# Packing the register tables of a gather ring: TensorE's slots and landed counts in one word of 30 bits, SyncE's reuse counts three to a word

## What is computed

```python
def _gnn_layer(x, row, col, W, b, g, beta):
    n = x.shape[0]
    neigh = x[col]
    agg = jax.ops.segment_sum(neigh, row, num_segments=n)
    deg = jax.ops.segment_sum(jnp.ones((row.shape[0],), x.dtype), row, num_segments=n)
    deg = jnp.maximum(deg, 1.0)[:, None]
    h = (x + agg / deg) @ W.T + b
    ...
    return jax.nn.silu(hn)
```

## Time and profile before

| what | value |
|---|---|
| median of 3 runs | 3740.51 us (3739.39 to 3745.12) |
| the profiled execution, its own time | 3739.08 us |
| its span, first to last instruction | 3737.3 us |
| TensorE busy / POOL busy | 2240.2 us (60%) / 1554.4 us (42%) |
| granted TensorE clock, mean over the span | 0.785 |

### The profile page before, as it was taken

One profiled execution on the slowest core, in us unless ns is written; L12 is line 12 of the kernel. 1 busy time (PEld: TensorE's weight loads), 2 busy tenths in 40 slices (PEclk: granted clock), 3 DMA queues, 4 the chain that ended last, 5 costly groups with the idle time before them and its releaser, 6 DMA issues.

```text
span 3737.3 us, 36443 instructions
## 1 busy us (share of the span) xinstructions
PE 2240.2 (60%) x9253; PEld 1681.5 (45%) x9253; DVE 1446.4 (39%) x3178; ACT 1600.0 (43%) x3874; POOL 1554.4 (42%) x1637
## 2 busy tenths in 40 slices
PE   0711456656656665568255666575666577079988
PEld 0411234445444454455144445454544465047766
DVE  8577512323333332215413323232333224866611
ACT  6000144445545454554344555454555453423333
POOL 0000166656666656630356656666666620400000
PEclk9955577878777877789577877787777788589979
DMA  4100133333333333321323323333332323200011
GB/s 155 57 0 0 30 89 93 94 90 97 90 92 93 97 87 90 88 64 58 118 85 92 94 88 99 93 92 90 92 94 85 90 72 135 95 26 0 0 82 55
DMA packets 100949, 293.32 MB, mean 78 GB/s; under 512 B 28161, under 2 KB 42319, under 8 KB 94538
## 3 DMA queue, kind: packets, MB, share of 16 engines
q0 software_dynamic: 75264, 205.62, 19.1%
q1 hardware_dynamic: 12524, 73.00, 5.2%
q10 hardware_dynamic: 13000, 12.80, 1.2%
HBM read 259.31 MB, written 32.00 MB: 78 GB/s over the span
## 4 chain that ended last, share of the span: by engine, by line
PE 35%; another core or an unknown queue 23%; DVE 22%; issue 9%; SPq 2%; DVEq 2%; DMA 2%; ACT 2%; POOL 0%; ACTq 0%; PEldq 0%; POOLq 0%
PE ps L929 17%; PE ps L1071 3%; DVE big L1463 3%; PE ps L1053 3%; DVE arena_a L1175 2%; PE ps L1140 2%; DVE arena_a L1176 2%; DVE nodes L1517 2%; PE ps L946 2%; PE ps L1013 1%; DVE big L1567 1%; PE ps L827 1%; DMA nodes<-x_rows 1%; ACT arena_b L592 1%
## 5 line engine op out<-in xcount | busy, mean ns | idle before, releaser
L495 POOL DMA_INDIRECT big<-table,arena_a x1568 | 1508.4, 962 | 1421.7 <-issue 447.0
L929 PE MATMUL ps<-big 128*125 x3968 | 1136.0, 448 | 920.3 <-DVE big L1463 778.6
L929 PEld LDWEIGHTS ps<-big 128*125 128x125 f32 x3968 | 876.7, 226 | 1153.5 <-issue 985.0
L1463 DVE TENSOR_TENSOR big<-ps,big 125x257 f32 x496 | 211.3, 426 | 1732.2 <-remote 976.8
L592 ACT ACTIVATE arena_b<-iota_row,arena_a 128x125 f32<-128x125 f32 x1984 | 601.4, 386 | 37.7 <-ACT nodes L633 14.0
L594 ACT ACTIVATE big<-arena_b,ones 128x1000 f32<-128x1000 f32 x248 | 280.2, 1130 | 22.6 <-remote 11.4
L622 ACT ACTIVATE nodes<-ps 128x750 f32<-128x750 f32 x50 | 39.9, 797 | 330.6 <-remote 328.6
L1517 DVE RECIPROCAL nodes<-nodes 125x512 f32<-125x512 f32 x50 | 167.7, 3353 | 1.7
L649 ACT ACTIVATE nodes<-ps 125x768 f32<-125x768 f32 x50 | 40.3, 806 | 289.8 <-remote 258.8
L946 PE MATMUL ps<-arena_b,nodes 128*125 128x384 f32 x400 | 159.4, 522 | 0.0
L615 ACT ACTIVATE nodes<-nodes 125x512 f32<-125x512 f32 x50 | 31.6, 631 | 260.3 <-issue 166.7
(11 more groups left out here) (362 smaller groups left out, 3018.4 us busy)
## 6 DMA issues: line engine op xcount, KB each, us to landing
big<-table,arena_a POOLq DMA_INDIRECT x1568
nodes<-in_x_dram SPq DMA_DIRECT2D x10, 1250.0 KB
table<-nodes SPq DMA_DIRECT2D x10, 1250.0 KB
nodes<-table SPq DMA_DIRECT2D x10, 1250.0 KB
nodes<-table ACTq DMA_DIRECT2D x50, 125.0 KB
mix_rows<-nodes ACTq DMA_DIRECT2D x50, 125.0 KB
big<-mix_rows SPq DMA_DIRECT2D x5, 1250.0 KB
x_rows<-nodes SPq DMA_DIRECT2D x5, 1250.0 KB
```

Of the source, the lines that this page charges most:

```text
L495: pool.indirect_dma_start(gat[:, GRP * slot + k, 0:D], None, table[l], bass.IndirectOffsetOnAxis(ap=s_dst[:, n:n + 1], axis=0)).then_inc(s ...
L929: mm = pe.matmul(ps[0:PT, 4 + q % 2, 0:257], onehot[:, ROUND * (r % 2) + QS * k + n, :], gat[:, bass.ds(slots[QS * k + n], 1), :].squeeze( ...
L1463: dve.tensor_tensor(at, ps[0:PT, 4 + q % 2, 0:257].unsqueeze(1), at, ALU.add).then_inc(s("agg_added"), 1)
```

## The change

Per quad there is now one word of 30 bits: four ring places of five bits, and above them the landed count of ten. `need_row` and `free_row` hold one layer's numbers; the other layer's share is added to the register. TensorE loads 16 such words at once, at the start of every fourth round, and takes each place out with a shift and a mask. SyncE's table has three counts of eight bits to a word, and 16 words (48 groups) to a load. The order of the engines' work stays as it was.

```diff
@@ -192,10 +192,12 @@
         s_row, o = carve(arena_a, o, [NSL])
         assert o <= 2 * NCK * P - NQ // PACK
         slot_row, o = carve(arena_a, 2 * NCK * P, [NSL], I32, 1)
-        need_row, o = carve(arena_a, o, [2, NQ], I32, 1)
+        quad_row, o = carve(arena_a, o, [NQ], I32, 1)
+        need_row, o = carve(arena_a, o, [NQ], I32, 1)
         tile_row, o = carve(arena_a, o, [NQ], F32, 1)
         pack_row, _ = carve(arena_a, 2 * NCK * P - NQ // PACK, [NQ // PACK], I32, 1)
-        free_row, o = carve(arena_a, o, [2, NGRP], I32, 1)
+        free_row, o = carve(arena_a, o, [NGRP], F32, 1)
+        free_words, o = carve(arena_a, o, [(NGRP - 2) // 3], I32, 1)
         assert o <= 4750 - 5 * (NT + 1)
         away, _ = carve(arena_b, 0, [GRP, PT])
 
@@ -402,13 +404,15 @@
             for l in range(2):
 
                 tell_landed(l, 0)
-                for first in range(0, NGRP - RG, 16):
-                    _, quads_before = nc.values_load_multi_w_load_instructions(
-                        free_row[0:1, l, first:first + 16], [mybir.EngineType.SP], min_val=1, max_val=2 * NQ,
-                        skip_runtime_bounds_check_because="a sum of clamped counts, held to one or more by a maximum before it is stored")
-                    for grp in range(first, min(first + 16, NGRP - RG)):
+                for first in range(0, NGRP - RG, 48):
+                    _, words = nc.values_load_multi_w_load_instructions(
+                        free_words[0:1, first // 3:first // 3 + 16], [mybir.EngineType.SP], min_val=1, max_val=(1 << 24) - 1,
+                        skip_runtime_bounds_check_because="three sums of clamped counts of eight bits, each held to one or more by a maximum")
+                    for grp in range(first, min(first + 48, NGRP - RG)):
                         tell_landed(l, grp + 1)
-                        sp.wait_ge(s("agg_made"), quads_before[grp - first])
+                        k = (grp - first) % 3
+                        quads_before = (words[(grp - first) // 3] >> (8 * k)) & 255
+                        sp.wait_ge(s("agg_made"), (quads_before + NQ * l).with_bounds(min_val=1, max_val=2 * NQ))
                         sp.sem_inc(s("slots_free"), 1)
                 for grp in range(NGRP - RG + 1, NGRP):
                     tell_landed(l, grp)
@@ -910,24 +914,28 @@
             for l in range(2):
                 pe.wait_ge(s("agg_added_credit"), l + 1)
 
-                def products(r, l=l):
-                    _, slots = nc.values_load_multi_w_load_instructions(
-                        slot_row[0:1, r * ROUND:(r + 1) * ROUND], [mybir.EngineType.PE], min_val=0, max_val=RG * GRP - 1,
-                        skip_runtime_bounds_check_because="five bits of a number")
-                    _, needs = nc.values_load_multi_w_load_instructions(
-                        need_row[0:1, l, r * (ROUND // QS):(r + 1) * (ROUND // QS)], [mybir.EngineType.PE], min_val=1, max_val=2 * NGA,
-                        skip_runtime_bounds_check_because="a chunk's number plus one, held to the tile's last by a minimum")
+                quad_words = []
+
+                def products(r, l=l, quad_words=quad_words):
+                    first = r * (ROUND // QS)
+                    if first % 16 == 0:
+                        _, loaded = nc.values_load_multi_w_load_instructions(
+                            quad_row[0:1, first:min(first + 16, NQ)], [mybir.EngineType.PE], min_val=1 << 20, max_val=(1 << 30) - 1,
+                            skip_runtime_bounds_check_because="four slots of five bits, and above them a chunk's number plus one, of ten")
+                        quad_words[:] = loaded
                     for k in range(ROUND // QS):
+                        word = quad_words[(first + k) % 16]
+                        slot = lambda n: ((word >> (5 * n)) & (RG * GRP - 1)).with_bounds(min_val=0, max_val=RG * GRP - 1)
                         q = r * (ROUND // QS) + k + NQ * l
                         if k * QS % GRP == 0:
                             pe.wait_ge(s("onehot_ready"), 2 * r + k * QS // GRP + 1 + NSG * l)
-                        pe.wait_ge(s("landed"), needs[k])
+                        pe.wait_ge(s("landed"), ((word >> 20) + NGA * l).with_bounds(min_val=1, max_val=2 * NGA))
                         if q >= 2:
 
                             pe.wait_ge(s("agg_added"), q - 1)
                         for n in range(QS):
                             mm = pe.matmul(ps[0:PT, 4 + q % 2, 0:257], onehot[:, ROUND * (r % 2) + QS * k + n, :],
-                                           gat[:, bass.ds(slots[QS * k + n], 1), :].squeeze(), start=(n == 0), stop=(n == QS - 1))
+                                           gat[:, bass.ds(slot(n), 1), :].squeeze(), start=(n == 0), stop=(n == QS - 1))
                         mm.then_inc(s("agg_made"), 1)
 
                 def mix_slot(i, l=l):
@@ -1420,12 +1428,21 @@
                                               op0=ALU.mult, op1=ALU.add))
             do.mark(dve.tensor_scalar(slot_row, chunk_row, -1.0, None, ALU.add))
             last_of_quad = chunk_row.rearrange("p (q c) -> p q c", c=QS)[:, :, QS - 1]
-            for l in range(2):
-                do.mark(dve.tensor_scalar(need_row[:, l, :], last_of_quad, float(NGA * l), None, ALU.add))
-                do.mark(dve.tensor_scalar(free_row[:, l, :], ps[0:1, 3, 3 * P:3 * P + NGRP], 1.0, float(NQ * l), ALU.max, ALU.add))
+            do.mark(dve.tensor_copy(need_row, last_of_quad))
+            do.mark(dve.tensor_scalar(free_row, ps[0:1, 3, 3 * P:3 * P + NGRP], 1.0, None, ALU.max))
             do.wait()
-            link(dve.tensor_scalar(slot_row, slot_row, RG * GRP - 1, None, ALU.bitwise_and))
-            link(dve.tensor_copy(pack_row, in_word(tile_row, 0)))
+            do.mark(dve.tensor_scalar(slot_row, slot_row, RG * GRP - 1, None, ALU.bitwise_and))
+            do.mark(dve.tensor_scalar(need_row, need_row, 20, None, ALU.logical_shift_left))
+            do.mark(dve.tensor_copy(pack_row, in_word(tile_row, 0)))
+            in_free = lambda k: free_row[:, 0:NGRP - 2].rearrange("p (w c) -> p w c", c=3)[:, :, k]
+            do.mark(dve.scalar_tensor_tensor(out=in_free(1), in0=in_free(2), scalar=256.0, in1=in_free(1), op0=ALU.mult, op1=ALU.add))
+            do.wait()
+            in_quad = lambda n: slot_row.rearrange("p (q c) -> p q c", c=QS)[:, :, n]
+            do.mark(dve.scalar_tensor_tensor(out=free_words, in0=in_free(1), scalar=256.0, in1=in_free(0), op0=ALU.mult, op1=ALU.add))
+            for n in (2, 1, 0):
+
+                link(dve.scalar_tensor_tensor(out=in_quad(n), in0=in_quad(n + 1), scalar=float(RG * GRP), in1=in_quad(n), op0=ALU.mult, op1=ALU.add))
+            link(dve.tensor_tensor(quad_row, in_quad(0), need_row, ALU.bitwise_or))
             dve.sem_inc(s("rows_ready"), 1)
             dve.wait_ge(s("pairs_made"), 1)
             dve.wait_ge(s("halves_ready"), 1)
```

## The result

The change made the kernel slower: a median of **3775.7 us** (3772.4 to 3782.5, four runs) against 3739.95 us (3739.04 to 3745.12, four runs) for the kernel before. The ratio is 1.0099, 95% interval 1.0086 to 1.0112, so 36 us, where 290 us of gain were forecast. It is the third rival's side, at the lower end of its 3776 to 3848.

A forecast was written before the change was run, and what follows sets the result against it. POOL's waits for ring places, blamed on TensorE's register loads, were taken as the bound: 3740.5 - 301.1 + 10.6 = 3450.0 us. The range was 3312 to 3600; faster by more than 0.2% had 90%, no difference 6%, slower 4%.

The forecast's parts named there:

- third rival: TensorE's path: added register arithmetic slows the kernel while holds stay unchanged; 36 to 107 us, so 3776 to 3848; 4%.
- What bounds the kernel: POOL's gathers in both layers: 108 waits for a ring place, 427.8 us, are all that stops POOL.
- The ceiling: POOL gathering without waits: at most 427.8 us gained, 3313 us.
- What starts a hold: TensorE register load during gathers delays its later semaphore increments until traffic pauses (a hold); each hold costs POOL a wait.
- The main term: POOL's waits: one of 3.96 us per remaining load, 32 in all, 126.7 us left; 301.1 us gained.
- counterexample: TensorE's load at 1527.5 us, in a POOL pause of 4.71 us, was followed by no hold; taken as support.
- holds come from something else that each round has: Such as the mix slot; only loads' own time counts: gain 0 to 144 us, 4%, or no difference, 6%.
- The loads' own time: TensorE's sequencer: 178.1 us of loads becomes about 34, 144 us less, counted as 0 since the array covers it.
- Register arithmetic: TensorE, 8 or 9 operations a quad at 55 ns: mostly hidden, 10.6 us added over 32 waits, at most 32.
- The prediction's condition for the price: Within a TensorE quad, arithmetic costs only if a slot's operations pass 0.46 us; expected 0.165 us.
- The slower rival: Register arithmetic in TensorE's path, holds unchanged: 108 waits x 2 quads x 0.165 to 0.5 us, 3776 to 3848; 4%.
- SyncE and VectorE: SyncE's fewer loads and VectorE's table operations: both hidden, 0 us; bounds 18 us gain and 1.6 us once.

The follow-up runs named there:

- s1_sync_part: SyncE's part of the change alone (reuse counts three to a word), with extra count masks, against the kernel before: 3721.7 us, 1.0011, on a chip with holds.
- a1_second_chip: The whole change again, with an extra mask on each counted wait, against the kernel before: 3766.9 us, 1.0127, on a chip with holds.
- n8: Kernel before, all loads kept, plus masks and value-neutral register arithmetic ahead of each product: 3763.5 us, 1.0128, with holds; 3333.1 us, 1.0019, without.
- k1: Kernel before with ring places, landed and reuse counts as constants, so without their register loads or arithmetic: 3710.5 us, 0.9978, on a chip with holds.
- b1: Kernel before plus only a mask on each table count before a wait: 3328.5 us, 0.9999, on a chip without holds.
- l2: Masked kernel before, meant to execute TensorE's two loads twice each round; the program still ran 248 loads: 3329.2 us, 0.9998, on a chip without holds.
- t1: TensorE's part of the change alone (30-bit words, no SyncE part), with masks, against the kernel before: 3764.7 us, 1.0116, on a chip with holds.
- a2: Masked change, meant to compute ring places ahead of each quad's waits; the arithmetic stayed in place: 3329.7 us, 1.0003 against the kernel before, without holds.
- p2: Kernel before, with masks, POOL waiting after every second group of gathers until it lands: 3506.8 us, 1.0539, on a chip without holds.

## Why the prediction was wrong, point by point

**What bounds the kernel: right.** The waits of POOL for a ring place carry most of the difference between kernels on chips with holds. From s1_sync_part to a1_second_chip the span grows by 36.6 us and these waits grow by 35.2; from s1 to n8, on another chip, by 40.6 and 38.5; between the two kernels of the study by 43.4 and 35.5. The ceiling, 427.8 us of waits, was also right, for the chips without holds show it: 3329 against 3313.

**What starts a hold: the step that failed.** The prediction said that a register load by TensorE while gathers are in flight makes its later increments wait. The main term, 301.1 us of gain from 124 loads becoming 32, rests on that. With 32 loads there are 112 waits; with none (k1) 106, and VectorE waits 998.4 us for "remote"; with 248 on a chip without holds (b1), no hold. What the runs show in the place of the load is the gather stream: the longer it has run, the more of TensorE's signals come late, and they are let go some 3 us after it stops. The prediction's evidence was one load just ahead of one hold and one counterexample in a pause of POOL. But a load occurs in each of 124 rounds, so one is found near each hold, and the counterexample had the property that matters anyway: it lay in a pause of the gathers. Two events of each round were confused, load and stream. The prediction even held the rival in hand ("holds come from something else that each round has") and gave it 10% with its two forms; the traffic itself, which it described as what ends a hold, was never weighed as what makes one.

**The loads' own time: right** as far as is shown: taking all loads and their register arithmetic away (k1) gains 0.22%, 7 us, on a chip with holds. That is a bound on the loads' price and far from the 144 us of sequencer time. No run changed the loads alone, since l2 did not double them.

**Register arithmetic: the number right, the price wrong under the stream.** Seven operations a quad for the places and one for the count came, of 36 ns where 55 were taken. But in holds some 600 of TensorE's register operations, new ones and old, take 0.7 us each, 13 times the 0.055 us taken, while TensorE's queue is still allowed to work ahead. The prediction's condition for the price, that the operations of a slot stay under the 0.46 us of its two records, was met everywhere but there, where two or three held operations stand between the records of one product and the next. It put them at 10.6 us in 32 waits; the waits of POOL grew by 35.5.

**The slower rival: right in side; that its 36 us are the 36 measured is luck.** It has "register arithmetic in TensorE's path, with the holds unchanged" and 36 us at its lower end, and t1 and n8 show that arithmetic as the cause. Its sum was 216 quads at 0.165 us each. The trace has instead a few long ones: 63 quads of over 4 us, of which 26 end within a pause of POOL. It was given 4%, because the operations were priced at their normal length, which rows 9 showed, in a kernel in which none is held.

**SyncE and VectorE: right.** s1 gives plus 0.11% (0.01 to 0.20), some 4 us, with the masks in it. The four loads that are left take 3.4 us each, and 36 of SyncE's new operations are held over 0.2 us, 23 us together, in s1. VectorE's tables left no trace in the start of the gathers: the first is at 442.9 us before and at 441.9 us after.

**What stays open.** Why TensorE's signals are late under the gather stream, why only on some chips, and what a held register operation waits for. That the two are one thing, a path out of the sequencer that takes one item in 0.7 us while gathers run and fills up, fits the traces: the slow operations come in holds (580 of 625), and only in the kernels with 12 to 13.5 register operations a quad on TensorE (none is held in those with 5 or fewer). So does a count in the traces of chip 10: of TensorE's signals due 4 to 8 us into a gather stream, 122 of 264 were late in k1 (no register operation a quad), 152 of 272 in s1 (5), 163 of 281 in a1 and 181 of 286 in t1 (13.5 each). It is argued, not shown. What moving the arithmetic does was never tested, since the program of a2 has it in the old place, and whether a pause in the stream lets signals go (p2) was not seen on a chip with holds. Nor was any run made to see whether the profiler's own records have a part in it. The Trainium skill, in its page "NOTIFIC — the notification-queue block", section "10. Constraints, capacities, measured rates", states that an implicit record costs the engine nothing and that at least 6.6 million records a second went through; the page's section "7.1 Overflow: three behaviours, one of which stalls the engine" says that the block's internal pipeline holds its producers back rather than lose a record. The first would speak against records as the cause, the second leaves it possible, and no run here shows either.

## What to carry to other kernels

A thing that occurs once in each round stands beside every wait of the round; before a term of 300 us is built on it, look for waits without it, and weigh the other events of the round that the counterexample shares. An engine's register instruction has the price of its worst neighbourhood: where the trace shows an engine's signals late, price added instructions of its queue by what lateness does to them, not by their quiet length, and expect that fewer loads bought with more arithmetic is a bad trade there. Where a chain has a large share of an "unknown queue" on one core, time the kernel on more than one chip before explaining it. And before reading an experiment's time, count in its trace the instructions that it was to add or move: two kernels here looked different in their source and ran as the same program.

## What the runs showed of the hardware

- The same kernel took 3717 to 3740 us on one kind of chip and 3328 to 3329 us on another, 12% apart, each steady within 0.6% on its chip. The kernel before has 97 waits of VectorE's addition for "remote" on the first kind, b1_counts_masked none on the other.
- Under a stream of indirect gathers, on a chip with holds, TensorE's semaphore increments due 8 us or more after the stream's start come almost all late (288 of 292 in the kernel before), by 9 us in the median and up to 22, and are let go 3 us after its last gather.
- There, register operations of TensorE that take 36 to 61 ns elsewhere are held for 0.7 us each: 625 to 727 of them in the kernels with 12 to 13.5 register operations a quad, none in those with 5 or fewer. Of SyncE's ALU operations 36 to 56 take over 0.2 us in the kernels with its part of the change.
- TensorE's register loads have no part in making the signals late: k1_constants has none in the gather stretches, and 106 waits of POOL for a place as against 107 in s1_sync_part on the same chip.
- On a chip without holds, 96 waits of POOL for its own gathers' landing cost 209.8 us, but the span grew by only 177 us (p2_pauses against b1_counts_masked): the gaps between gathers shrank from 478.4 to 450.0 us beside them.
